# The last two units of a conditional residual kernel in eight 32x64 tiles, with copies of 128x512 and stores of half units by SP

## The chip, the cores and the metric

The kernel runs on one core of a Trainium2 chip. The metric is the time of one execution on the device in microseconds (us); the median over several runs is compared. A profiled execution gives a trace beside it: its span runs from the first to the last instruction, and its time is the span plus what lies around it.

## The reference

128 batches of 64 x 512 values (`x`) go through two layers. Each layer picks one 64 x 64 matrix for each batch by an index, multiplies and adds the result to its input:

```
def layer(x, index, weights):
    w = weights[index]
    return jnp.einsum('bct,bcd->bdt', x, w)
x = x + layer(x, itok_B_0_7, L0_cond_weights)      # 8 matrices to pick from
x = x + layer(x, itok_B_1_198, L1_cond_weights)    # 200 matrices to pick from
return x
```

All is float32. `x` and the result are 16.78 MB each.

## The kernel before, in words

The two layers are folded into one matrix for each batch, M = (I + W0)(I + W1), so that `x` is read once and multiplied once. The 128 batches are 16 units of 8, a unit is two slots of 4 batches. A slot of `x` lies in SBUF as 128 partitions (4 batches x 32) of 1,024 values: each partition holds two neighbouring rows of 512 (index j) of one batch, 4 KB in a piece. `xy` has room for all 32 slots, so no load waits for room.

SP issues all loads of `x` at the start: one DMA for a unit (units 0 and 1 in part by slots), then waits for the stores at its end. ACT issues the stores, one for each unit, the last unit in two halves; a store is placed in ACT's program behind its copies of the next slot. POOL gathers the W1 matrices and copies the W0 matrices that each batch picks. These beginnings end about 22 us into the span.

From there PE runs blocks of units (`BLOCKS`: units 0 and 1 alone, then two at a time). For block k, `products(k + 1)` first makes the matrices M of the next block in 64x32 tiles; DVE and ACT (`copy_m`) take them out of PSUM, and a mask spreads them to block-diagonal 64x128 matrices for two batches (`m_diag`). Then `apply(k)` multiplies: a slot is 4 matmuls (2 halves of the partitions, 2 values of j) of 64 rows by 128 columns on 512 values; the two halves are two tiles of the array. A slot's result takes two PSUM banks, and three slots have room (`Y_RING`); `apply` waits before slot s until slot s - 3 is copied out. DVE and ACT each copy half of a slot (`copy_y`), in two copies of 64x512, back to the slot's own place in `xy`, with two output rows of one batch in a partition again. What sets the order of all this is the order in which the program is written, with semaphores between the engines (`s_x` for a unit of `x`, `s_y_psum`, `s_y_v` and `s_y_s` for a slot, `s_out` for a unit that is stored).

A float32 matmul appears in the trace as two records, each with its weight load.

Of the kernel before, what the change touches and what calls it, by code (L numbers as in the profile page):

```python
# [5 lines left out]
def bass_cond_residual_kernel(  # L6
# [5 lines left out]
    w1_dram: bass.AP,  # L12
    out_dram: bass.AP,
):

# [10 lines left out]
    fp32 = mybir.dt.float32  # L28
# [5 lines left out]
    P = 2 * C  # L34
# [8 lines left out]
    ROWS = S0 * C // P  # L43

    BLOCKS = [(0, 1), (1, 1)] + [(v, 2) for v in range(2, UNITS, 2)]
    M_COLUMNS = 4
    M_RING = 8

# [14 lines left out]
    QUARTERS = [slice(r * Q, (r + 1) * Q) for r in range(SLOT)]  # L63

    x_view = x_dram.rearrange("(s b) (p j) t -> (b p) s (j t)", b=SLOT, j=J)
    out_view = out_dram.rearrange("(s b) (q i) t -> (b q) s (i t)", b=SLOT, i=J)

    ctx = ExitStack()
    with ctx:  # L69
        def sb(name, shape, dt):  # L70
            return ctx.enter_context(nc.sbuf_tensor(name, shape, dt))
# [8 lines left out]
        w1 = sb("w1", [P, UNITS * SLOT, C], fp32)  # L80
        w0b = sb("w0b", [P, UNITS * SLOT, C], fp32)
        m_diag = sb("m_diag", [P, 2, M_RING, J, P], fp32)
        ident = sb("ident", [P, P], fp32)
        mask = sb("mask", [P, 2], fp32)
        cond = sb("cond", [B, 1], i32)
# [32 lines left out]
        @block.sync  # L118
        def _(sp):
            def load(s, n):  # L120
                sp.dma_start(xy[:, s:s + n, :], x_view[:, s:s + n, :]).then_inc(s_x[s // 2], 16)

            sp.dma_start(cond[:, :], cond_dram.rearrange("(b o) -> b o", o=1)).then_inc(s_cond, 16)
            load(0, 2)
            load(2, 1)

            sp.wait_ge(s_w0b_early, EARLY * UNIT)
            load(3, 1)
            for v in range(2, UNITS):
                load(2 * v, 2)  # L130
            for v in range(UNITS):
                sp.wait_ge(s_out[v], 32 if v == UNITS - 1 else 16)

        @block.gpsimd
        def _(pool):
# [24 lines left out]
        @block.tensor  # L160
        def _(pe):
            pe.wait_ge(s_ident, 1)
            pe.wait_ge(s_w0_rows, 16)
            for z in range(ROWS):
                last = nc.tensor.transpose(w0_psum[:, z * P:(z + 1) * P], w0_rows[:, z, :], ident[:, :])  # L165
            last.then_inc(s_w0_turned, 1)
            for n in range(TICKS):
                pe.wait_ge(s_tick, n + 1)
                for z in range(WARM):
                    nc.tensor.transpose(psum[0:C, z, 0:P], w0_rows[:, z, :], ident[:, :])  # L170


            pe.wait_ge(s_w1_plus, 1)
            for n in range(TURNS):
                if n >= W1_RING:

                    before = n - W1_RING
                    pe.wait_ge((s_w1_v, s_w1_s)[before % 2], 2 * (before // 2 + 1))
                for z in range(TURN):
                    last = nc.tensor.transpose(psum[0:C, n % W1_RING, z * B:(z + 1) * B],  # L180
                                               w1_rows[:, :, n * TURN + z], ident[:, :])
                last.then_inc(s_w1_turned, 1)

            def products(k):

                first, n = BLOCKS[k]
                if first + n <= EARLY:
                    pe.wait_ge(s_w0b_early, UNIT * (first + n))
                else:
                    pe.wait_ge(s_w0b, UNIT * (first + n - EARLY))  # L190
                if k >= 2:

                    pe.wait_ge(s_m_v, 2 * k)
                    pe.wait_ge(s_m_s, 2 * k)
                for v in range(first, first + n):
                    for j in range(J):
                        for r in range(SLOT):
                            for odd, rows in enumerate(HALVES):
                                at = (v % M_COLUMNS * J + j) * C
                                last = nc.tensor.matmul(psum[QUARTERS[r], M_BANKS[k] + odd, at:at + C],  # L200
                                                        w0b[rows, v * SLOT + r, j * Q:(j + 1) * Q],
                                                        w1[rows, v * SLOT + r, :], start=True, stop=True)
                last.then_inc(s_m_psum, 1)

            def apply(k):

                first, n = BLOCKS[k]
                pe.wait_ge(s_m_v, 2 * (k + 1))
                pe.wait_ge(s_m_s, 2 * (k + 1))
                for s in range(2 * first, 2 * (first + n)):  # L210
                    v, odd = s // 2, s % 2
                    pe.wait_ge(s_x[v], 32 if v == 1 else 16)
                    if s >= Y_RING:

                        pe.wait_ge(s_y_v, 2 * (s - Y_RING + 1))
                        pe.wait_ge(s_y_s, 2 * (s - Y_RING + 1))
                    for j in range(J):
                        for h, rows in enumerate(HALVES):
                            last = nc.tensor.matmul(psum[:, 2 * (s % Y_RING) + h, :],  # L219
                                                    m_diag[rows, odd, v % M_RING, j, :],  # L220
                                                    xy[rows, s, j * T:(j + 1) * T],
                                                    start=j == 0, stop=j == J - 1)
                    last.then_inc(s_y_psum, 1)

            pe.wait_ge(s_w1_v, TURNS)
            pe.wait_ge(s_w1_s, TURNS)
            products(0)
            for k in range(len(BLOCKS)):
                if k + 1 < len(BLOCKS):
                    products(k + 1)  # L230
                apply(k)

        def copy_w1(eng, copy, done, n):

# [6 lines left out]
        def copy_m(eng, scale, done, odd, k):  # L241
# [9 lines left out]
            for b in range(2):  # L251
                scale(to[:, b, :, :, :],  # L252
                      psum[:, M_BANKS[k] + odd, at:at + n * J * C].rearrange("q (w e i) -> q w i e", i=J, e=Q),
                      mask[:, b:b + 1]).then_inc(done, 1)

        def copy_y(eng, copy, done, i, s):

            eng.wait_ge(s_y_psum, s + 1)
            for h, rows in enumerate(HALVES):
                copy(xy[rows, s, i * T:(i + 1) * T], psum[HALVES[i], 2 * (s % Y_RING) + h, :]).then_inc(done, 1)  # L260
# [7 lines left out]
        def copies(eng, copy, scale, w1_done, m_done, y_done, odd):  # L268
            for n in range(odd, TURNS, 2):
                copy_w1(eng, copy, w1_done, n)  # L270
            eng.wait_ge(s_mask, 2 * SLOT)
            copy_m(eng, scale, m_done, odd, 0)
            copy_m(eng, scale, m_done, odd, 1)
            for k, (first, n) in enumerate(BLOCKS):
                for s in range(2 * first, 2 * (first + n)):
                    copy_y(eng, copy, y_done, odd, s)
                    if odd and s % 2 == 0 and s > 0:

                        store(s - 2, 2)
                if k + 2 < len(BLOCKS):  # L280
                    copy_m(eng, scale, m_done, odd, k + 2)

        @block.vector
# [33 lines left out]
        def _(act):  # L317
# [7 lines left out]
                    act.wait_ge(s_tick, n)  # L325
                nc.scalar.copy(w1[:, 0:ROWS, :], w0_rows[:, :, :]).then_inc(s_tick, 1)  # L326
            copies(act, nc.scalar.copy, nc.scalar.mul, s_w1_s, s_m_s, s_y_s, 1)
            store(SLOTS - 2, 1)
            store(SLOTS - 1, 1)


# [24 lines left out]
```

## Time and profile before

| | |
|---|---|
| time, median of 3 runs | 92.88 us (92.76 to 93.39) |
| time of the profiled execution | 92.78 us |
| its span | 91.0 us |
| PE busy | 78.5 us (86%) |
| DVE busy | 61.8 us (68%) |
| ACT busy | 58.6 us (64%) |
| moved by DMA | 35.93 MB, 395 GB/s in the mean |
| mean granted TensorE clock | 0.989 |

Times in the rows are us from the span's start unless marked ns. Busy time of an engine is the time in which it has an instruction under way; matmuls overlap, so that a busy PE is not one at its peak. "DMA share" is the mean busy share of the core's 16 DMA engines; as packets overlap a little it can be over 1. A queue (q1 is SP's, q10 ACT's, q0 POOL's gather) has a part on each of these 16 engines. A packet is one contiguous piece of a DMA or the small write that closes the DMA's part on an engine.

### The profile page before, as it was taken

The page shows a single profiled execution, that of the slowest core. Times are in us where ns is not written, and L with a number is a line of the kernel's source. Part 1 is how long each engine was busy: PE and PEld are TensorE (multiplying, and loading weights), DVE is VectorE, ACT ScalarE, POOL GpSimd, SP SyncE. Part 2 cuts the span into 40 slices and gives each one's busy share as a digit, 9 for nine tenths or more (in the row PEclk, how much of TensorE's full clock was granted, in tenths as well). Part 3 has the DMA queues.
Part 4 walks back from the last instruction along what each step waited for, and adds up shares of the span by engine and source line. Part 5 has one row for each costly group of instructions (what it writes and reads, how often), then busy time and mean ns, then how long its engine had stood idle before and what let it go on. Part 6 is the DMA issues. An engine that isn't in the chain of part 4 may idle for free.

```text
span 91.0 us, 2427 instructions
## 1 busy us (share of the span) xinstructions
PE 78.5 (86%) x890; PEld 44.7 (49%) x890; DVE 61.8 (68%) x127; ACT 58.6 (64%) x117; POOL 23.4 (26%) x119
## 2 busy tenths in 40 slices
PE   0499939994999999999999999999999999999200
PEld 0389929983554544364454445445454544444000
DVE  1087008995288888796887878788777888778700
ACT  2899806886276767585777667677666777577500
POOL 3400029999999959300000000000000000000000
PEclk9999999999999999999999999999999999999995
DMA  0999989999999999999999999999999999999993
GB/s 9 334 411 421 461 342 427 412 412 407 411 411 402 412 400 414 409 421 420 418 418 414 423 420 418 416 418 421 423 407 423 418 418 421 421 414 376 414 420 140
DMA packets 9181, 35.93 MB, mean 395 GB/s; under 512 B 721, under 2 KB 850, under 8 KB 9042
## 3 DMA queue, kind: packets, MB, share of 16 engines
q1 hardware_dynamic: 4512, 16.78, 46.3%
q10 hardware_dynamic: 4514, 16.91, 45.8%
q0 software_dynamic: 144, 2.10, 5.4%
q8 instruction: 7, 0.11, 0.5%
q14 instruction: 4, 0.03, 0.1%
HBM read 19.01 MB, written 16.78 MB: 393 GB/s over the span
## 4 chain that ended last, share of the span: by engine, by line
PE 70%; DMA 13%; DVE 9%; issue 1%; DVEq 1%; ACTq 0%; POOLq 0%
PE psum L219 62%; DMA w_rows<-in_L_cond_weights_dram,cond 10%; DVE w L238 7%; PE psum L200 7%; DMA subjects<-in_itok_B_dram 2%; DVEq L69 1%; DVE xy L260 1%; PE psum L180 1%; DVE m_diag L252 1%; ACTq L318 0%; DVE w_rows L313 0%; POOLq L149 0%; DVEq L244 0%
## 5 line engine op out<-in xcount | busy, mean ns | idle before, releaser
L219 PE MATMUL psum<-xy,m_diag 64*128 64x512 f32 x256 | 57.1, 596 | 0.5 <-DVE m_diag L252 0.5
L260 DVE COPY xy<-psum 64x512 f32<-64x512 f32 x64 | 43.7, 683 | 13.2 <-PE psum L219 12.2
L260 ACT COPY xy<-psum 64x512 f32<-64x512 f32 x64 | 37.2, 581 | 19.8 <-PE psum L219 19.0
L219 PEld LDWEIGHTS psum<-xy,m_diag 64*128 64x128 f32 x256 | 24.8, 187 | 27.1 <-issue 25.7
L157 POOL COPY w0b<-w0t 64x64 f32 x112 | 21.6, 235 | 11.0 <-DMA w_rows<-in_L_cond_weights_dram,cond 8.5
L200 PEld LDWEIGHTS psum<-w,w0b 64*32 64x32 f32 x512 | 5.6, 105 | 6.4 <-issue 3.8
L238 ACT COPY w<-psum 64x256 f32<-64x256 f32 x16 | 5.8, 364 | 4.1 <-PE psum L180 3.1
L180 PE MATMUL psum<-ident,w_rows 128*64 128x128 f32 x64 | 7.2, 274 | 1.4 <-DVE w_rows L313 1.4
L252 DVE TENSOR_SCALAR m_diag<-psum,mask 128x256 f32<-128x256 f32 (+1 forms) x18 | 7.3, 449 | 1.1 <-PE psum L200 0.9
L326 ACT COPY w<-w_rows 128x256 f32<-128x256 f32 x18 | 7.3, 405 | 0.9 <-DMA w_rows<-in_L_cond_weights_dram 0.3
L180 PEld LDWEIGHTS psum<-ident,w_rows 128*64 128x64 f32 x64 | 7.0, 152 | 1.6 <-DVE w_rows L313 1.6
L200 PE MATMUL psum<-w,w0b 64*32 64x64 f32 x512 | 6.9, 224 | 0.9 <-DVE w L238 0.9
L252 ACT ACTIVATE m_diag<-psum,mask 128x256 f32<-128x256 f32 (+1 forms) x18 | 7.0, 447 | 0.9 <-PE psum L200 0.7
L238 DVE COPY w<-psum 64x256 f32<-64x256 f32 x16 | 6.7, 417 | 1.2 <-PE psum L180 0.8
L170 PE MATMUL psum<-ident,w_rows 128*64 128x128 f32 x54 | 7.5, 308 | 0.0
L170 PEld LDWEIGHTS psum<-ident,w_rows 128*64 128x64 f32 x54 | 6.7, 128 | 0.7
L165 PE MATMUL psum<-ident,w_rows 128*64 128x128 f32 x4 | 1.0, 415 | 3.5 <-DMA w_rows<-in_L_cond_weights_dram 3.5
L297 DVE TENSOR_TENSOR w0t<-psum,ident 64x256 f32<-64x256 f32 x4 | 1.5, 411 | 3.4 <-PE psum L165 3.4
L313 DVE TENSOR_SCALAR w_rows<-w_rows 128x64 f32<-128x64 f32 x1 | 0.2, 225 | 4.3 <-DMA w_rows<-in_L_cond_weights_dram,cond 4.3
L326 ACT ACT_TABLE_LOAD x1 | 1.3, 1283 | 1.8 <-issue 1.8
L308 DVE COPY w0b<-w0t 64x64 f32 x16 | 2.1, 186 | 0.2
L165 PEld LDWEIGHTS psum<-ident,w_rows 128*64 128x64 f32 x4 | 0.5, 158 | 3.5 <-issue 3.5
(8 smaller groups left out, 2.3 us busy)
## 6 DMA issues: line engine op xcount, KB each, us to landing
xy<-in_x_dram SPq DMA_DIRECT2D x15, 1024.0 KB, 19.0
out_dram<-xy ACTq DMA_DIRECT2D x15, 1024.0 KB, 11.0
xy<-in_x_dram SPq DMA_DIRECT2D x2, 512.0 KB, 5.9
out_dram<-xy ACTq DMA_DIRECT2D x2, 512.0 KB, 4.3
w_rows<-in_L_cond_weights_dram ACTq DMA_DIRECT2D x1, 128.0 KB, 2.6
cond<-in_itok_B_dram SPq DMA_DIRECT2D x1, 0.5 KB, 2.4
subjects<-in_itok_B_dram ACTq DMA_DIRECT2D x1, 0.5 KB
w_rows<-in_L_cond_weights_dram,cond POOLq DMA_INDIRECT x1, 9.5
```

What stands on the lines that cost most here:

```text
L157: nc.gpsimd.tensor_copy(w0b[HALVES[odd], v * SLOT + r, :], w0t[HALVES[odd], bass.ds(picked[n] * C, C)]).then_inc(s_w0b, 1)
L165: last = nc.tensor.transpose(w0_psum[:, z * P:(z + 1) * P], w0_rows[:, z, :], ident[:, :])
L170: nc.tensor.transpose(psum[0:C, z, 0:P], w0_rows[:, z, :], ident[:, :])
L180: last = nc.tensor.transpose(psum[0:C, n % W1_RING, z * B:(z + 1) * B], w1_rows[:, :, n * TURN + z], ident[:, :])
L200: last = nc.tensor.matmul(psum[QUARTERS[r], M_BANKS[k] + odd, at:at + C], w0b[rows, v * SLOT + r, j * Q:(j + 1) * Q], w1[rows, v * SLOT + ...
L219: last = nc.tensor.matmul(psum[:, 2 * (s % Y_RING) + h, :], m_diag[rows, odd, v % M_RING, j, :], xy[rows, s, j * T:(j + 1) * T], start=j = ...
L238: copy(w1[rows, :, n * TURN:(n + 1) * TURN].rearrange("q (v r) k -> q v r k", r=SLOT), turned[:, odd, :, :, :]).then_inc(done, 1)
L252: scale(to[:, b, :, :, :], psum[:, M_BANKS[k] + odd, at:at + n * J * C].rearrange("q (w e i) -> q w i e", i=J, e=Q), mask[:, b:b + 1]).the ...
L260: copy(xy[rows, s, i * T:(i + 1) * T], psum[HALVES[i], 2 * (s % Y_RING) + h, :]).then_inc(done, 1)
L297: nc.vector.tensor_tensor(w0t[rows, :].rearrange("q (s j k y) -> q j s k y", s=S0, j=J, y=J)[:, j, :, :, :], turned[:, j, :, :, :], one[:, ...
L308: nc.vector.tensor_copy(w0b[HALVES[odd], v * SLOT + r, :], w0t[HALVES[odd], bass.ds(picked[n] * C, C)]).then_inc(s_w0b_early, 1)
L326: nc.scalar.copy(w1[:, 0:ROWS, :], w0_rows[:, :, :]).then_inc(s_tick, 1)
```

## The change

The last block (units 14 and 15, `LAST` = 14) is laid out differently, and the rest stays as it was.

- Loads: a slot of these units holds every other batch of the unit (o = 0 or 1) instead of four neighbouring ones. Its DRAM side is `last_x_view`, with 4 batches (r) at one stride and 32 rows (p) of 4 KB in each; SP issues one DMA for each slot, four in all.
- `products` writes the M of both units into one PSUM bank for each half, and `copy_m_last` takes them out with one plain copy of 64x512 on each engine, into `m_last`, without mask and without zeros.
- `apply_last` multiplies a slot in 8 matmuls in 32x64 tiles: a batch's 32 partitions by 64 columns. A slot uses two of the four row quarters and both halves of the columns, the next slot the other two quarters. The result has one output row of a batch in a partition.
- `copy_y_last`: DVE and ACT each copy one of a slot's two banks in one copy of 128x512, into the place of slots 0 to 3 in `xy`, after a wait for the stores of units 0 and 1.
- Stores: four, one for each slot, issued by SP behind its loads, with pieces of 2 KB. SP's last wait is for two stores of units 14 and 15 each.

```
+    LAST = BLOCKS[-1][0]
...
+    last_x_view = x_dram.rearrange("(v r o) (p j) t -> v o r p (j t)", r=SLOT, o=2, j=J)
+    last_out_view = out_dram.rearrange("(n o) c t -> (o c) n t", o=2)
...
+        m_last = sb("m_last", [P, UNITS - LAST, 2, J, C], fp32)
...
-            for v in range(2, UNITS):
+            for v in range(2, LAST):
                 load(2 * v, 2)
+            for v in range(LAST, UNITS):
+                for o in range(2):
+                    sp.dma_start(xy[:, 2 * v + o, :], last_x_view[v, o]).then_inc(s_x[v], 16)
+
+            for s in range(2 * LAST, SLOTS):
+                sp.wait_ge(s_y_v, 2 * (s + 1))
+                sp.wait_ge(s_y_s, 2 * (s + 1))
+                sp.dma_start(last_out_view[:, 2 * s:2 * s + 2, :],
+                             xy[:, s - 2 * LAST, :].rearrange("q (r t) -> q r t", r=2)).then_inc(s_out[s // 2], 16)
             for v in range(UNITS):
-                sp.wait_ge(s_out[v], 32 if v == UNITS - 1 else 16)
+                sp.wait_ge(s_out[v], 32 if v >= LAST else 16)
...
-                for v in range(first, first + n):
+                for v in range(LAST, UNITS if first == LAST else LAST):
+
+                    for o in range(2):
+                        for j in range(J):
+                            for h in range(2):
+                                for odd, rows in enumerate(HALVES):
+                                    r = 2 * odd + h
+                                    at = (((v - LAST) * 2 + o) * J + j) * C
+                                    last = nc.tensor.matmul(psum[QUARTERS[r], M_BANKS[k] + odd, at:at + C],
+                                                            w0b[rows, v * SLOT + 2 * h + o, j * Q:(j + 1) * Q],
+                                                            w1[rows, v * SLOT + 2 * h + o, :], start=True, stop=True)
+                for v in range(first, min(first + n, LAST)):
...
+            def apply_last():
+
+                pe.wait_ge(s_m_v, 2 * len(BLOCKS))
+                pe.wait_ge(s_m_s, 2 * len(BLOCKS))
+                for s in range(2 * LAST, SLOTS):
+                    v, half = s // 2, s % 2
+                    pe.wait_ge(s_x[v], 32)
+
+                    pe.wait_ge(s_y_v, 2 * (s - Y_RING + 1))
+                    pe.wait_ge(s_y_s, 2 * (s - Y_RING + 1))
+                    for j in range(J):
+                        for h in range(2):
+                            rows = QUARTERS[2 * half + h]
+                            for o, columns in enumerate(HALVES):
+                                last = nc.tensor.matmul(psum[columns, 2 * (s % Y_RING) + h, :],
+                                                        m_last[rows, v - LAST, o, j, :],
+                                                        xy[rows, 2 * v + o, j * T:(j + 1) * T],
+                                                        start=j == 0, stop=j == J - 1)
+                    last.then_inc(s_y_psum, 1)
...
+        def copy_m_last(eng, copy, done, odd):
+
+            k = len(BLOCKS) - 1
+            eng.wait_ge(s_m_psum, k + 1)
+            copy(m_last[HALVES[odd], :, :, :, :], psum[HALVES[odd], M_BANKS[k] + odd, :].rearrange(
+                "q (v o j e) -> q v o j e", v=UNITS - LAST, o=2, j=J)).then_inc(done, 2)
+
+        def copy_y_last(eng, copy, done, h, s):
+
+            eng.wait_ge(s_y_psum, s + 1)
+            eng.wait_ge(s_out[s // 2 - LAST], 16)
+            copy(xy[:, s - 2 * LAST, h * T:(h + 1) * T], psum[:, 2 * (s % Y_RING) + h, :]).then_inc(done, 2)
...
-                    copy_y(eng, copy, y_done, odd, s)
-                    if odd and s % 2 == 0 and s > 0:
+                    if s >= 2 * LAST:
+                        copy_y_last(eng, copy, y_done, odd, s)
+                    else:
+                        copy_y(eng, copy, y_done, odd, s)
+                    if odd and s % 2 == 0 and 0 < s <= 2 * LAST:
...
-                if k + 2 < len(BLOCKS):
+                if k + 3 == len(BLOCKS):
+                    copy_m_last(eng, copy, m_done, odd)
+                elif k + 3 < len(BLOCKS):
...
-            store(SLOTS - 2, 1)
-            store(SLOTS - 1, 1)
```

Two places in the order of the instructions carry most of the change. SP's program, first before; the names are the tiles and tensors, and the sizes are those of the SBUF side:

```order
L121 DMA xy<-in_x_dram 128x2x1024
L121 DMA xy<-in_x_dram 128x1024 x2
L121 DMA xy<-in_x_dram 128x2x1024 x14
L69 UNCONDITIONAL_BRANCH
```

and in the changed kernel, from the same place on:

```order
L130 DMA xy<-in_x_dram 128x2x1024
L130 DMA xy<-in_x_dram 128x1024 x2
L130 DMA xy<-in_x_dram 128x2x1024 x12
L142 DMA xy<-in_x_dram 128x1x1024 x4
L147 DMA out_dram<-xy 128x2x512 x4
L77 UNCONDITIONAL_BRANCH
```

Two whole loads became four of half the size, and the last four stores stand in SP's program behind them.

PE's program at its end, the last `products` and the matmuls around it (`L200` is `products`, `L219` `apply`; an array of 128x512 is the output), before:

```order
L219 MATMUL psum<-xy,m_diag 128x512 x16
L200 MATMUL psum<-w,w0b 32x64 x32
L219 MATMUL psum<-xy,m_diag 128x512 x32
L69 UNCONDITIONAL_BRANCH
```

and in the changed kernel:

```order
L248 MATMUL psum<-xy,m_diag 128x512 x16
L221 MATMUL psum<-w,w0b 32x64 x32
L248 MATMUL psum<-xy,m_diag 128x512 x16
L268 MATMUL psum<-xy,m_last 64x512 x32
L77 UNCONDITIONAL_BRANCH
```

The last 16 matmuls of four slots became 32 of half the columns and half the rows; nothing else moved on PE.

## Rows read from the trace of the kernel before

**Rows 1.** The page, span and engine table: busy us, share of the span, instructions.
```profile
span 91.0 us, 2427 instructions
PE 78.5 (86%) x890; PEld 44.7 (49%) x890; DVE 61.8 (68%) x127; ACT 58.6 (64%) x117; POOL 23.4 (26%) x119
```

**Rows 2.** The chain that ended last, its end: start us, us, what.
```profile
70.90 13.96 PE psum L219 x64
84.86 0.02 issue
84.88 0.68 DVE xy L260
85.56 0.71 DVEq L69
```

**Rows 3.** Windows: length, busy us (and instructions) by engine, clock, DMA share, GB/s.
```profile
48.00:68.00 20.00, 19.99 (x214) 9.72 (x212) 16.11 (x26) 13.86 (x26) 0.00 (x0) 1.00 1.02 418
68.00:80.00 12.00, 12.00 (x118) 5.61 (x116) 9.46 (x16) 8.08 (x15) 0.00 (x0) 1.00 1.03 420
80.00:83.00 3.00, 3.00 (x18) 1.35 (x16) 2.46 (x4) 2.05 (x4) 0.00 (x0) 1.00 1.03 416
83.00:84.00 1.00, 1.00 (x8) 0.53 (x6) 0.81 (x2) 0.81 (x2) 0.00 (x0) 1.00 0.84 344
84.00:89.00 5.00, 0.83 (x4) 0.00 (x1) 1.93 (x3) 1.51 (x3) 0.00 (x0) 1.00 1.01 410
89.00:89.50 0.50, 0.00 (x0) 0.00 (x0) 0.00 (x0) 0.00 (x0) 0.00 (x0) 0.50 0.78 311
89.50:90.00 0.50, 0.00 (x0) 0.00 (x0) 0.00 (x0) 0.00 (x0) 0.00 (x0) 0.50 0.28 115
```

**Rows 4.** The page's DMA queues: packets, MB, share of 16 engines.
```profile
q1 hardware_dynamic: 4512, 16.78, 46.3%
q10 hardware_dynamic: 4514, 16.91, 45.8%
q0 software_dynamic: 144, 2.10, 5.4%
```

**Rows 5.** The page's DMA issues: count, KB each, median us to landing.
```profile
cond<-in_itok_B_dram SPq DMA_DIRECT2D x1, 0.5 KB, 2.4
subjects<-in_itok_B_dram ACTq DMA_DIRECT2D x1, 0.5 KB
```

**Rows 6.** The loads' line L121: ns of an issue, first and last start; landing.
```profile
L121 SPq DMA_DIRECT2D xy<-in_x_dram x17: 333/1310/10435, 1.2 to 29.9; - x17
DMA to landing us min/median/max: 5.4/17.8/37.8
```

**Rows 7.** The same of the stores, by the tensor out_dram.
```profile
L266 ACTq DMA_DIRECT2D out_dram<-xy x17: 351/378/417, 29.1 to 86.3; - x17
DMA to landing us min/median/max: 4.2/10.4/15.3
```

**Rows 8.** The timeline near the end: start us, us, engine, line, what [idle before].
```profile
81.23 0.19 PEld L219 LDWEIGHTS psum<-xy,m_diag 64*128 64x128 f32 x2 [0.24 <-issue]
81.66 0.20 PEld L219 LDWEIGHTS psum<-xy,m_diag 64*128 64x128 f32 x2 [0.23 <-issue]
82.09 0.19 PEld L219 LDWEIGHTS psum<-xy,m_diag 64*128 64x128 f32 x2 [0.23 <-issue]
86.31 0.35 ACTq L266 DMA_DIRECT2D out_dram<-xy  x1
```

**Rows 9.** The page's costliest groups, three of them: busy us, mean ns of one.
```profile
L219 PE MATMUL psum<-xy,m_diag 64*128 64x512 f32 x256 | 57.1, 596 | 0.5 <-DVE m_diag L252 0.5
L260 DVE COPY xy<-psum 64x512 f32<-64x512 f32 x64 | 43.7, 683 | 13.2 <-PE psum L219 12.2
L200 PE MATMUL psum<-w,w0b 64*32 64x64 f32 x512 | 6.9, 224 | 0.9 <-DVE w L238 0.9
```

**Rows 10.** The timeline of one `products` on PE, by narrow windows.
```profile
70.04 0.86 PE L200 MATMUL psum<-w,w0b 64*32 64x64 f32 x64
```

More of the change, by code:

```diff
@@ L230, in _ @@
                     products(k + 1)
-                apply(k)
+                    apply(k)
+                else:
+                    apply_last()
         def copy_w1(eng, copy, done, n):
@@ L275, in copies @@
                 for s in range(2 * first, 2 * (first + n)):
-                    copy_y(eng, copy, y_done, odd, s)
-                    if odd and s % 2 == 0 and s > 0:
+                    if s >= 2 * LAST:
+                        copy_y_last(eng, copy, y_done, odd, s)
+                    else:
+                        copy_y(eng, copy, y_done, odd, s)
+                    if odd and s % 2 == 0 and 0 < s <= 2 * LAST:
                         store(s - 2, 2)
-                if k + 2 < len(BLOCKS):
+                if k + 3 == len(BLOCKS):
+                    copy_m_last(eng, copy, m_done, odd)
+                elif k + 3 < len(BLOCKS):
                     copy_m(eng, scale, m_done, odd, k + 2)
```

## The prediction

> **What bounds the kernel now.** I read the page's engine table first: PE is busy for 78.5 of 91.0 us [rows 1]. Then the chain that ended last: from 70.90 to 84.86 it is one unbroken run of 64 records of `apply`'s matmuls, and behind it stand only a DVE copy and the wait for the last stores [rows 2]. So PE looks like the bound. The windows by stretch say something else: from 48 us to 89 us the mean busy share of the 16 DMA engines is 1.01 to 1.03 and they move 410 to 420 GB/s, with one dip, 0.84 and 344 GB/s in 83 to 84 us [rows 3]. PE and the DMA engines are both full, and the tail after PE's end (84.86 to 91.0) is the DMA engines emptying what is queued. The reader is to see that any work that is added to a DMA engine lengthens the program, while work taken from PE in the last 7 us only feeds a queue that is already full.
>
> How fast is one engine? 420 GB/s over 16 engines is 26.2 GB/s, 156 ns for a row of 4,096 B. When most engines have stopped, the others are no faster: 311 GB/s at a share of 0.78 and 115 at 0.28 are 24.9 and 25.7 GB/s for an engine that works [rows 3]. Loads and stores share an engine evenly: after 68 us the windows add up to 8.9 MB, all of it stores, so 16.78 - 8.9 = 7.9 MB were stored before; the first store was issued at 29.1 [rows 7], and 37.5 us at about 415 GB/s are 15.6 MB, of which 7.9 is half. The last load was issued at 29.9 and took 37.8 us [rows 6]: all of `x` is in SBUF at 67.7, ten us before PE wants the last two units (its first slot of them starts near 77.8: 70.90 plus four slots of 1.72). Loads are hidden now with 10 us to spare.
>
> **The change, part by part.**
>
> *PE.* A slot is now 4 matmuls in two 64x128 tiles; each is two passes, and the weight loads come in pairs 0.43 us apart [rows 8], so a slot takes 4 x 0.43 = 1.72 us. Of the new slots each has 8 matmuls on four 32x64 tiles, again 4 passes a tile, 1.72 us; but two successive slots use different row quarters, so they can run side by side: two slots in about 1.72 + 0.16 = 1.88 us (a record lasts 596 ns against the pitch of 430, so the last pass ends 0.16 late) [rows 9]. That small tiles of different rows and columns run side by side is seen in `products`: 64 records in 0.86 us, 13 ns each, where one lasts 224 ns [rows 9, 10]. Worth 2 x (3.44 - 1.88), about 3 us of PE at the end, and by [rows 3] nearly all of it is hidden: the DMA engines can take back the dip of 83 to 84 us, 0.16 us.
>
> *Copies.* Two of 64x512 for each engine and slot become one of 128x512; 683 ns on DVE for 512 columns [rows 9] is taken for the new one as well. Saves 0.68 us a slot behind PE, hidden in the same way. The waits for s_out of units 0 and 1 are long past: the first store goes out at 29.1 and none takes over 15.3 us [rows 7]. `copy_m_last`, one copy in place of two scalings, can start when `products` of the last block ends at 70.9 [rows 10], and PE wants it at 77.8.
>
> *Stores.* 2 KB rows instead of 4 KB. From the queues [rows 4]: 46.3% x 16 x 91.0 us over 4,096 rows of 4 KB are 165 ns, 5.4% over 128 rows of 16 KB 614 ns; the straight line through both has about 15 ns that do not depend on size. An engine has 64 short rows in place of 32, so at most 0.5 us more, and not below nothing.
>
> *Loads of the last two units: the part that decides.* Before, one load's DRAM side is a list of 128 rows at one stride, and so is its SBUF side. The new view takes every other batch, so its DRAM side has an outer count of 4 (batches) with 32 rows in each, against 128 partitions on the SBUF side. What width does such a DMA get? The packet counts tell how wide the others are. Queue q1: 4,096 rows of x, 128 words of `cond` and 18 DMAs; 4,512 - 4,096 - 128 = 288 = 18 x 16, one closing packet for each engine of each DMA. Queue q10: 4,096 rows, 128 rows of `w0_rows`, one piece of `subjects`, 17 stores; 4,514 - 4,225 = 289 = 18 x 16 + 1. The odd one is `subjects`: outer count 1, one engine. `cond`, with as many bytes but 128 partitions, has sixteen and a landing of 2.4 us; `subjects` has no landing on the page at all [rows 4, 5]. So the width follows the outer count. For an outer count of 4 no row exists; the bounds are 4 engines and 16. I take 4, because where the outer count was small there were just as many engines as entries. That the four loads use the same four engines each time is assumed; if they moved on, it is the first rival.
>
> The Trainium skill (DMA: Bandwidth & Descriptors, "Why a DMA increments its semaphore by 16 and not by 1") says that the number of engines is the largest one up to 16 that divides the outermost count on both sides, as the instruction carries it, and that a DMA issued by SP takes the lowest-numbered ones. By it the four loads run on four engines, the same each time, and the sum is the one below; with sixteen it would be the first rival. The trace agrees as far as it goes (128 gives 16, 1 gives 1); no run here shows 4.
>
> **The sum, with four engines.** Each of the four engines gets 4 x 131,072 = 524,288 B of x for these two units, where it had 131,072; at 156 ns a row that is 15 us more for engines that have no idle time.
> - The two units took 2.1 MB at half of 418 GB/s, 10.0 us, so everything before them has landed at 67.7 - 10.0 = 57.7, on the last of sixteen engines.
> - From there the four engines give loads half of 26.2 GB/s: 524,288 B take 40.0 us. Half holds to the end: 5.8 MB (7.9 less 10 us at 209 GB/s) or 5.5 units are stored at 57.7, and the 8.5 units up to unit 13 put 557 kB in an engine's store queue. Unit 14 is in at 77.7, just in time for PE; unit 15 at 97.7 on the last engine. The last of four is a little earlier than the last of sixteen (engines end about 1 us apart at full rate [rows 3], 2 at half): 97.0.
> - PE stands from about 79.8 to 97.0 and its granted clock falls to the lower of its two levels: 0.50 (1.2 GHz) from 89.0 on now, with no matmul since 84.86 [rows 2, 3]. Slots 30 and 31 then take between 1.88 us (clock 1.00) and 3.8 us (0.50); nearer the upper end, as it may rise on the way: 3.4. 100.4.
> - Two DVE copies of 0.68 one after the other: 101.8.
> - SP issues the last store; landing 4.2 us later as the shortest now [rows 7] (2.4 us of `cond` is the lower bound). The four engines still have 1.2 us of old stores and 2.5 us of unit 14 from 97.0 on, done before it. 106.0.
> - From the last landing to the end of the span 0.5 us as now (86.31 + 4.2 against 91.0) [rows 8]. 106.5.
> - Around the span lie 92.78 - 91.0 = 1.8 us. The profiled execution's 92.78 is within 0.1 of the median of 92.88. **108.3 us.**
>
> Bounds: landing 95.7 to 97.7, PE 1.9 to 3.8, store 3.7 to 4.2, short rows 0 to 0.2: 105.0 to 109.6.
>
> **Rivals.**
> - *Full width (not slower).* The loads run on 16 engines, or on another four each time. For it: an SBUF side of 128 as everywhere else; against: `subjects`. Then x lands at 67.7 as now, PE gains 3 us and the DMA engines decide: 92.78 - 0.16 + 0.3 (short rows) = 92.9. It decides only near full width: with 14 engines each would have 149,800 B instead of 131,072, 0.7 us more, with 8 it would be 5 us. Chance 0.10. Even here over 1% faster would need the DMA engines to lose idle time that they do not have: 0.02 of it.
> - *Four engines, and the two last slots do not run side by side.* For it: PE takes work in order and a tile's second pass waits for its first; against: the 13 ns of `products`. At a low clock 2 x 3.44 in place of 3.4: 111.8. Chance 0.10.
> - *Four engines, loads ahead.* The four get more than half of their engines for x, or are engines that run ahead, and the clock is up again at once: landing near 94, PE 1.9: 103.8. Against it: the even share above. Chance 0.10.
> - The forecast itself: 0.70.
>
> **How the numbers follow.** 108.3 is the likeliest. The forecast's bounds hold 0.70; the range goes on from them to 104.0 and 111.5, close to the third and the second rival, and so takes in about half of each: 0.80. About 1% is what a measurement of this kernel can tell from no change: slower by more than that is every case with four engines, 0.90, less a little for a slower load that is hidden after all: 0.89; within 1% 0.09; faster 0.02.
>
> **What would show it.** Queue q1 with 4,096 + 1,024 + 128 + 16 x 16 + 4 x 4 + 4 x 16 = 5,584 packets (5,632 at full width). A DMA busy share that falls to about a quarter, some 105 GB/s, from about 82 us to 97 us, where it is 1.0 now. PE waiting some 17 us at `apply_last`'s second unit for `xy<-in_x`, and PEclk at 0.50 behind it. Slots 28 and 29 together in about 1.9 us show the tiles side by side. The forecast is wrong if the four loads of 512 KB land as early as 68 us; the step that then failed is the width.

## The result and the profile after

The changed kernel takes 107.03 us (median of 6 runs, 106.96 to 107.22), the kernel before 92.88 us (6 runs, 92.54 to 93.39) beside it: a ratio of 1.153, with a 95% interval of 1.149 to 1.156. The prediction said 108.3 us, between 104.0 and 111.5. The profiled execution of the changed kernel took 107.03 us, its span 105.2 us, 14.2 us more than [rows 1]. Some executions of a kernel run in a slower state, over 1.5% above its fastest, and medians and ratios here leave these out (three runs of experiment 6 and a few of the kernel before).

First the page of the changed kernel: span, engines (busy us, share of the span, instructions), the granted clock and the moved GB/s in 40 slices, and the two queues that carry the loads (q1) and most stores (q10): packets, MB, share of 16 engines.

```profile
span 105.2 us, 2493 instructions
PE 78.0 (74%) x922; PEld 44.4 (42%) x922; DVE 58.7 (56%) x122; ACT 55.9 (53%) x112; POOL 23.5 (22%) x119
PEclk9999999999999999999999999999999755555595
GB/s 36 373 439 467 358 419 417 399 409 409 408 406 389 417 414 414 420 417 420 420 420 422 408 417 422 406 386 218 405 313 291 398 322 106 106 104 103 106 248 203
q1 hardware_dynamic: 5584, 18.88, 45.1%
q10 hardware_dynamic: 3954, 14.81, 34.8%
```

PE is as busy as before (78.0 against 78.5 us in [rows 1]); the span grew by time in which little moves: five slices near 105 GB/s, with the clock at 0.5 around them. Queue q1 has the 5,584 packets that were worked out for four engines; full width would have been 5,632.

The windows of the changed kernel, in the columns of [rows 3] (stretch, length, busy us of PE, PEld, DVE, ACT, POOL, clock, DMA share, GB/s):

```profile
72.00:76.00 4.00, 4.00 (x22) 1.75 (x19) 2.73 (x4) 2.32 (x4) 0.00 (x0) 1.00 0.72 294
80.00:88.00 8.00, 0.00 (x0) 0.00 (x0) 1.16 (x2) 1.03 (x2) 0.00 (x0) 0.67 0.76 303
88.00:95.00 7.00, 0.00 (x0) 0.00 (x0) 0.00 (x0) 0.00 (x0) 0.00 (x0) 0.50 0.26 105
95.00:99.00 4.00, 3.23 (x32) 1.32 (x32) 0.00 (x0) 0.00 (x0) 0.00 (x0) 0.50 0.26 103
99.00:100.00 1.00, 0.63 (x8) 0.00 (x0) 0.42 (x1) 0.43 (x1) 0.00 (x0) 0.64 0.26 107
100.00:101.00 1.00, 0.00 (x0) 0.00 (x0) 0.87 (x2) 0.64 (x2) 0.00 (x0) 1.00 0.24 98
101.00:104.00 3.00, 0.00 (x0) 0.00 (x0) 0.00 (x0) 0.00 (x0) 0.00 (x0) 0.85 0.95 357
104.00:105.20 1.20, 0.00 (x0) 0.00 (x0) 0.00 (x0) 0.00 (x0) 0.00 (x0) 0.50 0.04 15
```

From 88 to 101 us a share of 0.24 to 0.26 is what four engines out of sixteen come to, each at its usual 26 GB/s. They finish unit 15 and then, from 95.8 us on, older stores, while the other twelve have nothing to do. The timeline near the end of the changed kernel (start us, us, engine, line, what [idle before]) and the landing of the four last stores:

```profile
77.81 2.07 PE L268 MATMUL psum<-xy,m_last 32*64 32x512 f32 x32
95.77 3.87 PE L268 MATMUL psum<-xy,m_last 32*64 32x512 f32 x32 [15.89 <-DMA xy<-in_x_dram]
99.58 1.29 DVE L318 COPY xy<-psum 128x512 f32<-128x512 f32 x2 [18.41 <-issue]
```

```profile
L147 SPq DMA_DIRECT2D out_dram<-xy x4: 372/382/1024, 80.6 to 100.9; - x4
DMA to landing us min/median/max: 3.2/4.9/21.0
```

Unit 14 (slots 28 and 29) starts at 77.81 with no wait for `x`. Unit 15 holds PE for 15.89 us. SP's second store of unit 14, issued at 81.2, takes 21.0 us to land: it too needs the four engines that are behind. The last store of all, issued at 100.9, lands 3.9 us later, at 104.8:

```profile
L147 SPq DMA_DIRECT2D out_dram<-xy x1: 372/372/372, 100.9 to 100.9; - x1
DMA to landing us min/median/max: 3.9/3.9/3.9
```

### The profile page after: what moved, and what is told of

It is laid out like the page before. It is cut to its first block, busy times and chain, and to the rows that moved or that the text cites. A ratio compares the mean times of both kernels' runs of the same rounds, so it can differ in the third digit from the quotient of the medians.

```text
span 105.2 us, 2493 instructions
## 1 busy us (share of the span) xinstructions
PE 78.0 (74%) x922; PEld 44.4 (42%) x922; DVE 58.7 (56%) x122; ACT 55.9 (53%) x112; POOL 23.5 (22%) x119
## 3 DMA queue, kind: packets, MB, share of 16 engines
q1 hardware_dynamic: 5584, 18.88, 45.1%
## 4 chain that ended last, share of the span: by engine, by line
SPq 42%; DMA 29%; issue 19%; DVE 3%; DVEq 2%; PE 1%
DMA xy<-in_x_dram 26%; SPq L142 23%; SPq L130 19%; DMA w_rows<-in_L_cond_weights_dram 2%; DVE w0b L377 1%; DVE w0t L366 1%; DVEq L77 1%; PE psum L183 1%; DVEq L371 0%; DVEq L377 0%; DVE xy L318 0%; DVEq L360 0%
## 5 line engine op out<-in xcount | busy, mean ns | idle before, releaser
L248 PE MATMUL psum<-xy,m_diag 64*128 64x512 f32 x224 | 50.2, 596 | 0.5 <-DVE m_diag L303 0.5
L324 DVE COPY xy<-psum 64x512 f32<-64x512 f32 x56 | 38.3, 684 | 12.2 <-PE psum L248 11.3
L324 ACT COPY xy<-psum 64x512 f32<-64x512 f32 x56 | 32.5, 581 | 18.2 <-PE psum L248 17.5
L248 PEld LDWEIGHTS psum<-xy,m_diag 64*128 64x128 f32 x224 | 21.8, 187 | 23.2 <-issue 21.9
L268 PE MATMUL psum<-xy,m_last 32*64 32x512 f32 x64 | 5.9, 834 | 15.9 <-DMA xy<-in_x_dram 15.9
L318 DVE COPY xy<-psum 128x512 f32<-128x512 f32 x4 | 2.6, 686 | 19.0 <-issue 19.0
L318 ACT COPY xy<-psum 128x512 f32<-128x512 f32 x4 | 2.2, 587 | 19.3 <-PE psum L268 18.5
L268 PEld LDWEIGHTS psum<-xy,m_last 32*64 32x64 f32 x64 | 2.2, 172 | 18.7 <-DMA xy<-in_x_dram 16.8
L303 DVE TENSOR_SCALAR m_diag<-psum,mask 128x256 f32<-128x256 f32 (+1 forms) x16 | 6.4, 446 | 1.1 <-PE psum L229 0.9
L229 PE MATMUL psum<-w,w0b 64*32 64x64 f32 x448 | 6.0, 224 | 0.9 <-DVE w L289 0.9
```

What stands on the lines that cost most here:

```text
L248: last = nc.tensor.matmul(psum[:, 2 * (s % Y_RING) + h, :], m_diag[rows, odd, v % M_RING, j, :], xy[rows, s, j * T:(j + 1) * T], start=j = ...
L268: last = nc.tensor.matmul(psum[columns, 2 * (s % Y_RING) + h, :], m_last[rows, v - LAST, o, j, :], xy[rows, 2 * v + o, j * T:(j + 1) * T], ...
L303: scale(to[:, b, :, :, :], psum[:, M_BANKS[k] + odd, at:at + n * J * C].rearrange("q (w e i) -> q w i e", i=J, e=Q), mask[:, b:b + 1]).the ...
```

## The experiments

Two questions were open after the result. What costs: by the theory of **width**, four engines carry the four loads and the rest follows; its rival is **shape**, that the new matmuls, copies or short store rows cost. And what sets the end: either the **chain** landing, PE, copies, store (the sum of the prediction was written so) or the **work of the four engines**, whatever PE does.

**1. The old compute with the new loads (e2_narrow_only).** Only the loads of units 14 and 15 are those of the change.

```
 before.py
...
-for v in range(2, UNITS):
+for v in range(2, UNITS - 2):
     load(2 * v, 2)
+for v in range(UNITS - 2, UNITS):
+    for o in range(2):
+        sp.dma_start(xy[:, 2 * v + o, :], last_x_view[v, o]).then_inc(s_x[v], 16)
...
-pe.wait_ge(s_x[v], 32 if v == 1 else 16)
+pe.wait_ge(s_x[v], 32 if v == 1 or v >= UNITS - 2 else 16)
```

> The kernel before with one edit: units 14 and 15 are loaded by the four new loads (every other batch, outer count 4), so that the batches of these two units meet the wrong matrices; all else is as before, tiles, copies and stores too. Theory (loads alone): unit 15 lands near 96 us, two slots of 64x128 tiles behind it at a granted clock of 0.5 take 5.4 to 6.9 us, copies 1.4, last store 4.2: 109 us (107.5 to 110.5). Rival (the loads are hidden, the rest of the change costs): 93 us.

Measured: 107.1 us (1 run), against 92.84 of the kernel before on that chip, and below the 107.5 to 110.5 that the chain gave. Its windows (columns as above), PE's last stretch in the timeline, and queue q1:

```profile
88.00:97.00 9.00, 3.79 (x10) 1.73 (x12) 0.00 (x0) 0.00 (x0) 0.00 (x0) 0.56 0.26 105
```

```profile
93.21 6.68 PE L223 MATMUL psum<-xy,m_diag 64*128 64x512 f32 x16 [9.55 <-DMA xy<-in_x_dram]
```

```profile
q1 hardware_dynamic: 4496, 16.78, 40.0%
```

With none of the new matmuls, copies or stores the whole loss is there, and 4,496 packets are [rows 4] less 2 x 16 for two wide loads and plus 4 x 4 for four narrow ones. Width holds, shape falls. One thing does not fit the chain: here PE resumes at 93.21 and needs 6.68 us in place of 3.87 after 95.77, so that it ends 0.25 us later than in the changed kernel, with other copies and stores behind it, and yet the span is the same 105.2 us. That unit 15 is in 2.6 us sooner fits a later start of the stores: in this run the granted clock is 0.50 in 14 to 16 us, where the changed kernel has 1.00, PE's first matmul of `apply` starts at 24.9 instead of 22.3, and the first store goes out at 31.4 instead of 28.8, which leaves the loads more of the engines.

**2. The change with an outer count of 8 and of 32 (e3_outer8, e4_outer32).** The DRAM side of each load takes eight runs of 16 rows, or 32 runs of 4, in place of four of 32. The bytes, the SBUF side and all else are the change's. The diff shows 8; the other has `g=32`.

```
 after.py
-last_x_view = x_dram.rearrange("(v r o) (p j) t -> v o r p (j t)", r=SLOT, o=2, j=J)
+last_x_view = x_dram.rearrange("b (p j) t -> (b p) (j t)", j=J).rearrange(
+    "(v g o p) f -> v o g p f", v=UNITS, g=8, o=2)
```

> The changed kernel with a DRAM side of 8 entries of 16 rows in each of the four loads (every other half batch, so the values of the last two units are not those of the reference), same bytes, same pieces of 4 KB. Theory (as many engines as the outer count has entries): eight engines, each with 262,144 B instead of 131,072, that is 32 rows of 156 ns or 5.0 us more on engines without idle time: 92.9 + 5.0 = 97.9 us (97.0 to 98.5); q1 with 5,248 + 16 x 16 + 4 x 8 + 4 x 16 = 5,600 packets; unit 15 lands near 77 us, in time for PE. Rival A (a DRAM side in two levels always gets four engines): 107 us. Rival B (four is special, eight is already enough): 93 us.

> The changed kernel with a DRAM side of 32 entries of 4 rows in each of the four loads (wrong values for the last two units again). It is still a list in two levels that can't be merged into one of 128. Theory: 32 entries give sixteen engines, 92.9 us (92.5 to 93.3), q1 with 5,632 packets, all landed near 68 us. Rival (a list in two levels is slow in itself, whatever its outer count, in the engines or in SP's issue): 105 to 107 us.

Measured: 97.81 us with 8 (1 run); 93.11 us with 32 (10 runs), a ratio of 1.003 (1.0015 to 1.0045) to before. Queue q1 and two windows of the kernel with 8, then of the one with 32:

```profile
q1 hardware_dynamic: 5600, 18.88, 49.6%
```

```profile
84.00:89.00 5.00, 0.00 (x0) 0.00 (x0) 0.00 (x0) 0.00 (x0) 0.00 (x0) 0.81 1.03 401
89.00:92.00 3.00, 0.00 (x0) 0.00 (x0) 0.00 (x0) 0.00 (x0) 0.00 (x0) 0.50 0.53 212
```

```profile
q1 hardware_dynamic: 5632, 18.88, 52.2%
```

```profile
83.00:84.00 1.00, 0.00 (x0) 0.00 (x0) 0.57 (x1) 0.45 (x1) 0.00 (x0) 1.00 1.03 416
84.00:89.00 5.00, 0.00 (x0) 0.00 (x0) 0.00 (x0) 0.00 (x0) 0.00 (x0) 0.56 1.03 397
```

The closing packets read 4 x 4, 4 x 8 and 4 x 16 above the same 5,568, and the DMA share of the tail is 0.26, 0.53 (eight of sixteen) and 1.03. An outer count of 4, 8 and 32 gets 4, 8 and 16 engines, and the time follows: +14.15, +4.97 and +0.27 us. The Trainium skill (DMA: Bandwidth & Descriptors, "Why a DMA increments its semaphore by 16 and not by 1") gives the largest count up to 16 that divides both outermost counts, 4, 8 and 16 here; the packet counts agree with each.

**3. The change with each load cut by batch (e1_split_loads).** Four loads of 32 rows each take the place of one, so that both sides have an outer count of 32.

```
 after.py
-sp.dma_start(xy[:, 2 * v + o, :], last_x_view[v, o]).then_inc(s_x[v], 16)
+for r in range(SLOT):
+    sp.dma_start(xy[QUARTERS[r], 2 * v + o, :], last_x_view[v, o, r]).then_inc(s_x[v], 16)
...
-pe.wait_ge(s_x[v], 32)
+pe.wait_ge(s_x[v], 32 * SLOT)
```

> The changed kernel with each of its four loads cut in four, one for each batch of the slot: 16 DMAs of 32 rows of 4 KB, DRAM side and SBUF side both a plain list of 32. Nothing else differs. Theory (the outer count of 4 keeps each load on four engines): now sixteen engines, unit 15 landed near 68 us, queue q1 with 4,096 + 1,024 + 128 + 16 x 36 = 5,824 packets, and 92.9 us (92.5 to 93.3), that is the 14.1 us are all gone and PE's saved 3 us are hidden behind full DMA engines. Rival (the tiles, the wait for the first units' stores, the short rows or SP's queue cost the time): 105 us or more, unit 15 may land early and PE or the copies then wait for something else.

Measured: 93.46 us (6 runs), ratio 1.0053 (1.0035 to 1.0070), a little above the 92.5 to 93.3 that was expected. The loss is gone, and the new PE work, copies and stores gain nothing. Queue q1 has sixteen loads of sixteen engines, 5,568 + 256 packets:

```profile
q1 hardware_dynamic: 5824, 18.88, 51.9%
```

**4. PE kept at work while it waits (e7_kept_busy).** The change with 34 matmuls more (`KEEP` is 34), whose results nobody reads, between slots 29 and 30, so that PE is at work until shortly before unit 15 lands.

```
 after.py
...
+if s == SLOTS - 2:
+    pe.wait_ge(s_m_v, 2 * len(BLOCKS))
+    for n in range(KEEP):
+        nc.tensor.matmul(psum[0:C, 6 + n % 2, :], m_diag[HALVES[n % 2], 0, 0, 0, 0:C],
+                         xy[HALVES[n % 2], 8, 0:T], start=True, stop=True)
```

> The changed kernel with 34 extra matmuls of 64x64 on 512 values in PE's program ahead of slot 30, into PSUM banks that nothing reads; they fill the wait for unit 15 from 79.9 to about 94.5 us, so that the granted clock should stay at 1.00. Slots 30 and 31 then take 2.1 us instead of 3.9. Theory A (the sum as it was predicted: landing of unit 15, PE, copies, last store, one after the other): 107.03 - 1.8 = 105.2 us. Theory B (four DMA engines have work without a pause until the end, and the last stores wait behind their older ones): 107.0 us (106.7 to 107.2), with PE's saved time lost in front of the stores.

Measured: 107.09 us (1 run). PE in the timeline, the end in the windows, and the landing of the last store, issued at 98.7:

```profile
80.00 14.81 PE L264 MATMUL psum<-xy,m_diag 64*64 64x512 f32 x68
95.29 2.23 PE L274 MATMUL psum<-xy,m_last 32*64 32x512 f32 x32 [0.48 <-DMA xy<-in_x_dram]
```

```profile
88.00:95.00 7.00, 6.81 (x32) 1.96 (x28) 0.00 (x0) 0.00 (x0) 0.00 (x0) 1.00 0.26 105
95.00:97.00 2.00, 1.71 (x32) 1.08 (x32) 0.00 (x0) 0.00 (x0) 0.00 (x0) 1.00 0.30 115
97.00:101.00 4.00, 0.53 (x12) 0.00 (x0) 1.29 (x2) 1.07 (x2) 0.00 (x0) 0.90 0.64 246
101.00:104.00 3.00, 0.00 (x0) 0.00 (x0) 0.00 (x0) 0.00 (x0) 0.00 (x0) 0.50 0.43 164
102.00:103.50 1.50, 0.00 (x0) 0.00 (x0) 0.00 (x0) 0.00 (x0) 0.00 (x0) 0.50 0.26 100
```

```profile
L148 SPq DMA_DIRECT2D out_dram<-xy x1: 373/373/373, 98.7 to 98.7; - x1
DMA to landing us min/median/max: 6.1/6.1/6.1
```

The last two slots take 2.23 us at a clock of 1.00 where they took 3.87 at 0.50, PE ends 2.1 us sooner (97.5 against 99.6), and the time does not move: Theory A, 105.2 us, is refuted. Up to the landing of unit 15 (95.29 against 95.77) this run is no slower than the changed kernel. The last store is issued 2.2 us sooner (98.7 against 100.9) and takes 2.2 us longer to land (6.1 against 3.9), so that both land at 104.8. In 101 to 104 us the changed kernel had all engines at work (0.95); here the share is 0.43, and in 102 to 103.5 us 0.26: most have ended, and as much as four engines carry is left. The end is the work of the narrow engines, not the chain through PE. This would explain the end of experiment 1 too, which was not tried apart.

**5. The short rows by themselves (e6_short_rows).** The kernel before with all its stores in 2 KB rows.

```
 before.py
-out_view = out_dram.rearrange("(s b) (q i) t -> (b q) s (i t)", b=SLOT, i=J)
+out_view = out_dram.rearrange("(n o) c t -> (o c) n t", o=2)
...
-nc.scalar.dma_start(out_view[:, s:s + n, :], xy[:, s:s + n, :]).then_inc(s_out[s // 2], 16)
+nc.scalar.dma_start(out_view[:, 2 * s:2 * (s + n), :],
+                    xy[:, s:s + n, :].rearrange("q s (i t) -> q (s i) t", i=J)).then_inc(s_out[s // 2], 16)
```

> The kernel before with all stores in pieces of 2 KB, as those of the last two units in the change (the rows go to other places of the output, so its order is not the reference's). It multiplies the price of the short rows by eight. Price from outer count 32's window of 84 to 89 us, 397 GB/s of short rows against 410 to 418 of long ones: 0.25 us for 2.1 MB. Theory (DMA engines are the bound from 13 us on): 16.8 MB cost 2.0 us (1.7 to 2.5), 94.8 us. Rival (PE is the bound until 84.9 us and hides it): at most the last 2 to 3 MB count, 93.2 us.

Measured: 93.84 us (2 runs), ratio 1.012 (1.0099 to 1.0141), between the two expectations. Its windows, and the landing of the loads on L121:

```profile
48.00:68.00 20.00, 19.91 (x212) 9.47 (x210) 15.55 (x26) 13.38 (x26) 0.00 (x0) 1.00 1.04 410
84.00:89.00 5.00, 1.25 (x6) 0.19 (x2) 2.31 (x4) 1.91 (x4) 0.00 (x0) 1.00 1.03 394
```

```profile
DMA to landing us min/median/max: 5.3/17.8/29.6
```

Against [rows 3], 410 GB/s in place of 418 while loads and stores are mixed, and 394 in place of 410 when stores go alone: 2 to 4% fewer bytes. Of the 16.8 MB the change makes 2.1 MB short, 5.1 us at 410 GB/s, so its short rows cost some 0.1 to 0.2 us: small, as taken. The landing was not expected, and is told at the end.

**6. The dip (e5_sp_half_stores).** The kernel before with its last four slots stored one by one by SP, as the change does, but in 4 KB rows. This should fill the dip of 83 to 84 us in [rows 3].

```
 before.py
+for s in range(SLOTS - 4, SLOTS):
+    sp.wait_ge(s_y_v, 2 * (s + 1))
+    sp.wait_ge(s_y_s, 2 * (s + 1))
+    sp.dma_start(out_view[:, s:s + 1, :], xy[:, s:s + 1, :]).then_inc(s_out[s // 2], 16)
...
-if odd and s % 2 == 0 and s > 0:
+if odd and s % 2 == 0 and 0 < s <= SLOTS - 4:
...
```

> The kernel before with one piece of the change: its last four slots are stored one by one by SP (in the old layout, pieces of 4 KB), ACT stores up to unit 13. Theory (the DMA engines set the end; the dip of 83 to 84 us is the only idle time to be had): the DMA share of that us goes from 0.84 to 1.0 and the time falls by 0.1 to 0.2 us, 92.7. Rival (PE's end and the last store's latency set the end): no change, 92.84, as PE and the last copies end where they did.

Measured: 92.86 us (9 runs), ratio 1.0020 (1.0006 to 1.0034). The theory missed. Its windows, and under them one of the kernel before:

```profile
83.00:84.00 1.00, 1.00 (x8) 0.53 (x6) 0.80 (x2) 0.81 (x2) 0.00 (x0) 1.00 1.01 414
86.00:89.00 3.00, 0.00 (x0) 0.00 (x0) 0.28 (x1) 0.07 (x1) 0.00 (x0) 1.00 0.96 392
89.00:89.50 0.50, 0.00 (x0) 0.00 (x0) 0.00 (x0) 0.00 (x0) 0.00 (x0) 0.76 0.52 213
```

```profile
86.00:89.00 3.00, 0.00 (x0) 0.00 (x0) 0.28 (x1) 0.06 (x1) 0.00 (x0) 1.00 1.02 414
```

The dip is filled (0.84 to 1.01), but the idle time only moves to the tail, where the share is 0.96 and 0.52 in place of 1.02 and 0.78 [rows 3]. A mean over sixteen engines does not say whether the one that ends last stood idle, and by the account of the work only that one is worth time; no view shows it.

**7. The change with its batches dealt anew (e8_mended).** To find whether the change can pay at all: each row quarter holds four neighbouring batches, so that a load goes to 32 partitions with an outer count of 32 and is again 512 KB in one DMA.

```
 after.py
-for v in range(LAST, UNITS):
-    for o in range(2):
-        sp.dma_start(xy[:, 2 * v + o, :], last_x_view[v, o]).then_inc(s_x[v], 16)
+for r in range(SLOT):
+    b = UNIT * (LAST + r % 2) + SLOT * (r // 2)
+    sp.dma_start(xy[QUARTERS[r], 2 * LAST:SLOTS, :], x_dram[b:b + SLOT].rearrange(
+        "n (p j) t -> p n (j t)", j=J)).then_inc(s_x[LAST], 16)
...
-pe.wait_ge(s_x[v], 32)
+pe.wait_ge(s_x[LAST], 16 * SLOT)
```

The factors that `products` picks and the rows that SP stores follow the new deal.

> The changed kernel with the batches of the last two units dealt to the slots in another way: a row quarter holds four neighbouring batches, one for each of the four slots. One load then has 32 partitions against a list of 32 rows times 4 batches, still four loads of 512 KB; tiles, copies and 2 KB stores as in the change, and the values are the reference's. Theory: sixteen engines, q1 with 5,632 packets, time as with outer count 32: 93.1 us, 0.2 to 0.3 % over the kernel before, as the short rows cost 0.25 and the dip gives 0.16 back. Rival (a load on 32 partitions at a time is slower): 93.5 or more, as with the sixteen split loads.

Measured: 93.49 us (5 runs), ratio 1.0082 (1.0069 to 1.0096). That is what the rival said, and not the 93.1 of the theory. As in experiment 3 the width is full (5,632 packets in q1). The loads of e4_outer32 go to 128 partitions, and its ratio is 1.0030 on another chip; e8's is 0.5% above it, and e1, on the same chip as e4, is 0.35 us above it. Both kernels with 32-partition loads are slower by 0.35 to 0.5 us; why is open.

**8. The start (e9_half_wait, e10_no_wait).** If the DMA engines are the bound, only an earlier start or less idle time can beat both kernels. SP waits before the load of slot 3 (its fourth DMA, with that of `cond`) for 16 early copies of `w0`; these runs halve that wait (the diff) and remove it, in the kernel before.

```
 before.py
-sp.wait_ge(s_w0b_early, EARLY * UNIT)
+sp.wait_ge(s_w0b_early, EARLY * UNIT // 2)
```

> The kernel before; SP's wait ahead of its fourth load is for 8 of the 16 early copies of W0 instead of all, so all later loads are issued some 0.8 us sooner. What is being looked for is a version that beats both kernels, at the other end of the span: the DMA share is 0.69 in 10.5 to 11.0 us and 0.86 to 0.92 in 11.5 to 12.5, 0.25 us of idle engines. Theory (the engines' work and idle time set the end): 0.1 to 0.25 us faster, 92.6. Rival (the gather shares its engines then, lands later, and every later step of PE with it): no change or up to 0.5 us slower.

> The kernel before without SP's wait ahead of the fourth load: its loads go out one behind the other from 1.2 us on and share the engines with the gather. Theory (as the half wait): no idle engines before 13 us, 0.1 to 0.25 us faster, 92.6, though the gather lands 3 to 5 us later and PE's start and end move by as much; PE's end at 84.9 has the 4 us of queued stores behind it. Rival (PE's later end moves the last stores as well): 2 to 4 us slower, 95 to 97.

Measured: 92.80 us (12 runs), ratio 0.9997 (0.9976 to 1.0018), and 96.27 us (6 runs), ratio 1.0369 (1.0343 to 1.0396); both as the rivals said. The chain of waits of the two, its last run of matmuls (first e9, then e10; start us, us):

```profile
71.90 13.96 PE psum L219 x64
```

```profile
75.01 13.96 PE psum L218 x64
```

It starts at 70.90 in [rows 2]. Earlier loads delay the gather of `w_rows`, whose landing goes from 9.5 us to 10.6 and 12.2, and with it all of PE's work: its last run of matmuls starts 1.0 and 4.1 us later. In e10 the gather accounts for 2.7 of the 4.1; PE's granted clock, 0.50 in 16 to 18 us where the kernel before has 1.00, would account for the rest. Then the stores come too late to keep the DMA engines full, 0.68 in 84 to 88 us:

```profile
16.00:18.00 2.00, 2.00 (x10) 1.68 (x11) 0.83 (x2) 0.17 (x1) 1.88 (x11) 0.50 1.03 414
84.00:88.00 4.00, 4.00 (x22) 1.82 (x20) 3.27 (x6) 2.87 (x6) 0.00 (x0) 1.00 0.68 261
```

The gather in the page's DMA issues (the tensor, the issuing queue, median us to landing), of the kernel before and of e10:

```profile
w_rows<-in_L_cond_weights_dram,cond POOLq DMA_INDIRECT x1, 9.5
```

```profile
w_rows<-in_L_cond_weights_dram,cond POOLq DMA_INDIRECT x1, 12.2
```

So the wait is worth 3.5 us, and halving it changes nothing that can be measured. No version here beats the kernel before.

## Why the prediction was right, point by point

The steps of its sum beside what the changed kernel shows:

| step | predicted | measured |
|---|---|---|
| packets of q1 | 5,584 | 5,584 |
| GB/s and share while PE waits | 105, a quarter | 105, 0.26 |
| slots 28 and 29 together | 1.88 us | 2.07 us |
| unit 15 is in | 97.0 us | 95.77 us (PE resumes) |
| slots 30 and 31 | 3.4 us (1.88 to 3.8) | 3.87 us at a clock of 0.50 |
| two copies | 1.4 us | 1.29 us |
| last store to its landing | 4.2 us | 3.9 us |
| from there to the end of the span | 0.5 us | 0.4 us |
| span | 106.5 us | 105.2 us |
| whole time | 108.3 us | 107.03 us |

- **The bound.** Right: the DMA engines are full from 48 to 89 us, and PE's saving is hidden [rows 3]. At full width (e4) PE ends at 82.76, 2.1 us sooner than in [rows 2], and the time is 0.27 us longer, where 92.9 was worked out and 93.11 measured. The other direction is not hidden: in e10 PE ends 4.1 us later, and the time is 3.5 us longer. The gain on PE was put at 3 us; the four slots took 4.80 us in place of 6.88, a gain of 2.1. The timeline of e4 (PE's four slots, and ACT's copies of the last two):

```profile
77.96 4.80 PE L269 MATMUL psum<-xy,m_last 32*64 32x512 f32 x64
...
81.73 0.59 ACT L319 COPY xy<-psum 128x512 f32<-128x512 f32 x1 [0.55 <-PE psum L269]
...
82.87 0.59 ACT L319 COPY xy<-psum 128x512 f32<-128x512 f32 x1 [0.55 <-PE psum L269]
```

  Slots 30 and 31 end 1.14 us apart, so they run side by side only in part. There are three PSUM slots, and slot 31 waits for the copies of slot 28, which would explain it; this was not tried apart. With the DMA engines full it did not matter.
- **The width.** Right, and the step that decides. It was assumed from the closing packets of `subjects` and `cond` [rows 4, 5]; e2 showed that the loads alone make the loss, e3 and e4 that the outer count sets the engines. That the four loads use the same engines is shown too: the share stays at 0.26 up to the end of unit 15, where loads on different engines would have shared the work out.
- **The landing.** The even share of an engine between loads and stores put unit 15 at 97.0, 1.2 us late. Unit 14 was in before 77.81, as needed. The share began to fall sooner than foretold, 0.72 in 72 to 76 us, and came down to a quarter later, from 88 to 101 us, where 82 to 97 was written. Which of the engines ran short in 72 to 76 us is in no view.
- **The clock.** Right in kind, and worth about what was said, just above the upper bound of 3.8: 3.87 us at 0.50 against 2.23 at 1.00 (e7). But it is worth nothing to the time.
- **The form of the sum.** Wrong, although its number was near. It added a chain: landing, PE, copies, store, as if the end waited for each. It counted 3.7 us of stores that the four engines had left when unit 15 was in, and held them to be done before the last store; in the trace they go on for at least 5.2 us (0.24 to 0.26 up to 101). e7 took 2.1 us out of that chain and e2 changed its parts; both ended at 107.1. That the chain ended beside the work in the changed kernel, and its sum so near the time, is luck. What sets the end is the account written one line above the chain: each of the four engines has 96 rows more, 15.0 us at 156 ns, and never stands idle. By it the time is 92.8 + 15.0 = 107.8. With eight engines the same account gives 32 rows and 5.0 us; measured 4.97. Of the 15.0 us, 14.15 were measured. Against e4, which differs from both in the width alone, they are 4.70 and 13.92 us, 6 and 7% less than the account, so the near hit of 4.97 is partly chance. What is missing is open; that these engines have less than the mean of other work would do it, and no view shows single engines.
- **The rivals.** Full width: 92.9 foretold, 93.1 to 93.5 where the runs gave it. Loads ahead, 103.8: the loads were ahead by 1.2 us only, and e7 shows that a faster PE behind them does not help. Slots not side by side, 111.8: refuted by the 2.07 us for slots 28 and 29.

## What to carry to other kernels

A DMA's price is read from the number of engines that carry it: multiply its rows by the time of a row on one engine, and add that to the most loaded engine when the engines are full. After a change of a DMA's view, compare the outer count of each side, and count the queue's packets: one closing packet for each engine of each DMA tells its width. And when the engine that is late never idles, sum its work, not the chain of waits that happens to end beside it: the chain here gave nearly the right number, and promised 1.8 us for e7, which returned nothing.

## What was not expected of the hardware

- **Row length sets the share between two queues.** With 2 KB rows in the store queue (e6) the last load landed 29.6 us after its issue in place of 37.8 [rows 6], with the same loads and 2% fewer bytes moved. If an engine takes a row from each queue in turn, 4 KB of load against 2 KB of store gives loads two thirds: the 15.6 - 7.9 = 7.7 MB of loads that the prediction's sum leaves outstanding take 7.7 / (0.667 x 410 GB/s) = 28.2 us. That is near, and was not tried with other lengths.
- **A queue left to four engines stays at their rate.** 105 GB/s over four is 26.2 each, no more than when all sixteen work at 420, so there is nothing to win back while twelve stand idle. The prediction read this from half a microsecond of the tail [rows 3]; here it holds over 13 us.
- **Loads to 32 partitions.** e1 and e8, both with full width, are 0.35 to 0.5 us slower than e4 with 128 partitions; the cause is open.
